# A two-layer transformer kernel: layer 1's cross attention and routing carried inside the full attention's steps

## The reference, cut to what matters

```python
h = _layernorm(x) * (1 + ca) + sa
x = x + ga * full_attention(h)            # 16 heads of 8, softmax over 1024 tokens
h = _layernorm(x) * (1 + cb) + sb
x = x + gb * ffn(h)

def ffn(hidden):                           # (S, B, H) = (4, 1024, 128)
    ln1 = layernorm(hidden) * w1 + b1
    q, k, v = split(ln1 @ qkv.T)           # 16 heads of 8 for q, 4 for k and v
    scores = einsum('sbhd,tbhd->bhst', q, k) / sqrt(8)      # over the leading axis, causal
    attn = einsum('bhst,tbhd->sbhd', softmax(scores), v)
    after = hidden + attn @ proj.T
    x = layernorm(after) * w2 + b2
    probs = softmax(x @ router.T)          # 8 experts, the best two taken
    ...                                    # gelu experts, weighted sum
    return after + moe_out
```

## Time and profile before

| What | Value |
|---|---|
| time, median of 3 runs | 2022.56 us (2022.13 to 2023.56) |
| the profiled execution | 2024.25 us, its span 2022.5 us |
| busy over the span | PE 1586.4, DVE 1386.9, ACT 1146.0, POOL 605.2 us |
| granted clock of PE, mean | 0.876 of full speed |
| full attention | 951.8 to 1632.7 us |
| double norm stage | 1633.9 to about 1694 us |
| cross and routing stage | 1696.5 to about 1871 us |
| experts and gather of layer 1 | 1871.4 to the end |

### The profile page before, as it was taken

One profiled execution on the slowest core, in us unless ns is written; L12 is line 12 of the kernel. 1 busy time (PEld: TensorE's weight loads), 2 busy tenths in 40 slices (PEclk: granted clock), 3 DMA queues, 4 the chain that ended last, 5 costly groups with the idle time before them and its releaser, 6 DMA issues. The chain is left out here.

```text
span 2022.5 us, 34560 instructions
## 1 busy us (share of the span) xinstructions
PE 1586.4 (78%) x11512; PEld 920.5 (46%) x11512; DVE 1386.9 (69%) x3531; ACT 1146.0 (57%) x2997; POOL 605.2 (30%) x670
## 2 busy tenths in 40 slices
PE   6799999999993399634999999999999953540780
PEld 3477877777772389622122222222222233440670
DVE  5655656656655164277999999999999656971653
ACT  3366666666662144343488888888888844210232
POOL 2133433633625377401001000100100011066574
PEclk8799999999996699866799999999999976555895
DMA  6144444411110467343000000000000000011664
GB/s 195 32 160 163 156 144 145 136 36 36 47 31 23 145 219 222 113 129 105 18 21 24 21 24 21 24 19 26 21 24 10 2 1 7 0 39 46 195 200 139
DMA packets 97805, 157.57 MB, mean 78 GB/s; under 512 B 18228, under 2 KB 64372, under 8 KB 97500
## 3 DMA queue, kind: packets, MB, share of 16 engines
q1 hardware_dynamic: 79900, 100.65, 17.1%
q0 software_dynamic: 17728, 54.71, 7.6%
HBM read 75.68 MB, written 63.49 MB: 69 GB/s over the span
## 5 line engine op out<-in xcount | busy, mean ns | idle before, releaser
L2106 DVE TENSOR_REDUCE q_max<-s_ps 128x1 f32<-128x1024 f32 x512 | 598.2, 1218 | 14.3 <-PE s_ps L1997 6.6
L2087 ACT ACTIVATE probs<-s_ps 128x512 f32<-128x512 f32 x1024 | 535.5, 603 | 124.9 <-PE s_ps L2018 124.7
L1997 PE MATMUL s_ps<-k_stack,q_stack 64*128 64x512 bf16 x1024 | 351.8, 397 | 17.5 <-PEq L99 9.1
L2018 PE MATMUL s_ps<-q_stack,k_stack 64*128 64x512 bf16 x1024 | 319.9, 385 | 20.1 <-ACT probs L2087 15.6
L2032 PE MATMUL o_ps<-probs,v_aug 128*32 128x512 f32 x2048 | 273.7, 607 | 0.7 <-ACT probs L2087 0.7
L2018 PEld LDWEIGHTS s_ps<-q_stack,k_stack 64*128 64x128 bf16 x1024 | 78.4, 94 | 334.4 <-ACT probs L2087 282.6
L1003 POOL TENSOR_TENSOR probs<-probs,p_rsum 128x512 f32<-128x512 f32 x128 | 132.9, 1039 | 311.5 <-DVE p_rsum L980 310.6
L883 ACT ACTIVATE probs<-s_biased,s_min 128x128 f32<-128x128 f32 (+1 forms) x512 | 197.7, 391 | 38.5 <-DVE s_min L974 37.1
L1638 POOL CAST neg_max_parts<-neg_max 16x128 bf16<-16x128 f32 x32 | 9.0, 281 | 475.0 <-DVE neg_max L2114 475.0
L748 PE MATMUL score_ps<-k_pad,q_bd 128*128 128x128 f32 x1024 | 146.0, 286 | 0.0
L974 DVE CUSTOM_DVE_ANT_0 s_biased<-score_ps,nbias 128x128 f32<-128x128 f32 (+1 forms) x512 | 115.7, 282 | 41.6 <-PE score_ps L748 40.4
(11 more groups left out here) (328 smaller groups left out, 2868.3 us busy)
## 6 DMA issues: line engine op xcount, KB each, us to landing
moe_rows<-zero_rows POOLq DMA_DIRECT2D x36, 975.0 KB, 5.9
moe0b_wblock<-in_L_ffn_blocks SPq DMA_DIRECT2D x39, 578.0 KB, 4.1
moe1b_wblock<-in_L_ffn_blocks SPq DMA_DIRECT2D x39, 256.0 KB
v_shift<-v_tiles SPq DMA_DIRECT2D x32, 256.0 KB, 3.4
v_shift<-v_tiles SPq DMA_DIRECT2D x32, 224.0 KB, 3.9
qk_parts_dram<-qk_parts SPq DMA_DIRECT2D x16, 384.0 KB, 2.6
q_stack<-qk_parts_dram SPq DMA_DIRECT2D x192, 32.0 KB
k_stack<-qk_parts_dram SPq DMA_DIRECT2D x192, 32.0 KB
```

The source lines that it names most:

```text
L1997: mm = nc.tensor.matmul(s1[u % 2][:, c * CH:(c + 1) * CH], qs[head_rows(m), quad % 4, j, qt * P:(qt + 1) * P], ks[head_rows(m), quad % 4, ...
L2018: nc.tensor.matmul(bank_of("exp", 4 * k + pos)[:], ks[head_rows(m), quad % 4, j, kt * P:(kt + 1) * P], qs[head_rows(m), quad % 4, j, half ...
L2087: nc.scalar.activation(pr[:, k % 2, HEADS[pos], :], bank_of("exp", n)[:], ACT.Exp).then_inc(sm["exp"], 1)
L2106: v.tensor_reduce(mx[:, h % 4, col:col + 1], s1[u % 2][:], AX.X, ALU.max).then_inc(sm["maxed"], 1)
```

## The change

`double_norm_stage` and `cross_route_stage` are removed. Their work becomes a class `BehindAttention`, made inside `full_attention_stage`, and every engine's loop over k gets a call `carried(k)`. For k in batch b (64 steps) it issues a part of the projection, the norms, the cross attention and the routing of batch b - 1, at fixed steps of the 64. Batch 3 follows behind the loop, in the same block. In detail:

- A `HalfNorm` replaces `Norm` and works on units of 4 tiles. In carried batches the odd tiles and the shift go to POOL.
- The cross attention of carried batches goes from DVE to POOL: the product (`score`), the sum over 8 as three halving additions, the totals and the weighted values. DVE keeps the maximum, the subtraction and the reciprocal. For batch 3 all of it is on DVE, in two halves of 4 tiles.
- Modulation of carried batches goes to POOL; for batch 3 it is on DVE.
- PE's turns, projections, logits and prefix counts use the ring of three `s2` banks: 18 further entries in `uses` a batch, 14 emptied by ACT and 4 by DVE.
- Logits and prefix counts are copied out of PSUM by ACT before DVE reads them.
- Scatters of a batch are spread over steps 61 to 70 after its batch's start of carrying (two a step, some in the next batch's steps); batch 3's 16 stand at the end.
- The weights are loaded by SP at the start of the attention stage (`C.load`). `q`, the scores and the products reuse spent buffers (`K.hT`, `K.mod_rows`).

More of the change, by code:

```diff
@@ L189, in affine @@
                                       ACT.Identity, bias=bias, scale=scale).then_inc(self.turn_read, 1)
[L192 to L281, removed]
@@ L1969, in split_max, with augment @@
                            nr[:])
-                wo.gate(pool)
-                for quad in range(NQ):
+                def augment(quad):
                     if quad >= 2:
@@ new lines, in total @@
+                def total(b):
+                    pool.wait_ge(C.exped, b + 1)
+                    if b == 0:
+                        g.tensor_copy(C.sm[:], C.sc[:, 0, :]).then_inc(C.totalled, 1)
+                    for t in range(1, b + 1):
+                        r = g.tensor_tensor(C.sm[:], C.sm[:] if t >= 2 else C.sc[:, 0, :], C.sc[:, t, :], ALU.add)
+                        if t < b:
+                            step(r)
+                        else:
+                            r.then_inc(C.totalled, 1)
@@ L1988, in _ @@
+                M1.wait_scattered(pool)
             @block.tensor
@@ L2225, in cross_route_stage @@
+class BehindAttention:
     QW, KW = H1 * HD1, KV2 * HD1
[L2226 to L2227 removed]
     R = H1 // KV2
[L2229 to L2501 removed]
@@ new lines, in attention_turned, with attention_product @@
+    def attention_turned(self, act, bank, u):
+        act.wait_ge(self.wo.turned, u + 1)
+        if u >= 2:
+            act.wait_ge(self.p_mm, u - 1)
+        self.nc.scalar.copy(self.aT[:, u % 2, :], bank[:]).then_inc(self.wo.t_out, 1)
+    def attention_product(self, pe, bank, u):
+        pe.wait_ge(self.wo.t_out, u + 1)
+        for i in range(CPT):
+            m = self.nc.tensor.matmul(bank[:, i * D:(i + 1) * D], self.aT[:, u % 2, i * P:(i + 1) * P],
+                                      self.wo.wg[:, u // 2, :], start=True, stop=True)
+        m.then_inc(self.wo.y_mm, 1)
@@ new lines, in project, with projected @@
+    def project(self, pe, bank, n):
+        pe.wait_ge(self.N2.turn_read, n // 2 + 1)
+        for i in range(2):
+            t = (2 * n + i) % TPB
+            m = self.nc.tensor.matmul(bank[:, i * QKV2:(i + 1) * QKV2], self.hT[:, t * P:(t + 1) * P], self.w[:],
+                                      start=True, stop=True)
+        m.then_inc(self.mm, 1)
+    def projected(self, act, bank, n):
+        act.wait_ge(self.mm, n + 1)
+        y = bank[:, 0:2 * QKV2].rearrange("p (t c) -> p t c", t=2)
+        if n % 4 == 0 and n >= 4:
+            act.wait_ge(self.below_max, n // 4)
+        self.nc.scalar.copy(self.q[:, 2 * n % TPB:2 * n % TPB + 2, :], y[:, :, 0:self.QW])
+        self.nc.scalar.copy(self.kv[:, :, 2 * n:2 * n + 2, :],
+                            y[:, :, self.QW:].rearrange("p t (a c) -> p a t c", a=2)).then_inc(self.qkv_out, 1)
@@ new lines, in exponentials, with out_turn, out_turned @@
+    def exponentials(self, act, b, ts, count):
+        act.wait_ge(self.below_max, count)
+        row = self.sc[:, 0:b + 1, self.columns(ts)]
+        self.nc.scalar.activation(row, row, ACT.Exp, scale=HD1 ** -0.5).then_inc(self.exped, 1)
+    def out_turn(self, pe, bank, u):
+        for i in range(CPT):
+            m = self.nc.tensor.transpose(bank[:, i * P:(i + 1) * P], self.at[:, u % 2 * CPT + i, :], self.K.ident[:])
+        m.then_inc(self.turned, 1)
+    def out_turned(self, act, bank, u):
+        act.wait_ge(self.turned, u + 1)
+        act.wait_ge(self.wo.y_mm, u + 1)
+        self.nc.scalar.copy(self.aT[:, u % 2, :], bank[:]).then_inc(self.t_out, 1)
@@ new lines, in out_product, with residual @@
+    def out_product(self, pe, bank, u):
+        pe.wait_ge(self.t_out, u + 1)
+        for i in range(CPT):
+            m = self.nc.tensor.matmul(bank[:, i * D:(i + 1) * D], self.aT[:, u % 2, i * P:(i + 1) * P], self.wp[:],
+                                      start=True, stop=True)
+        m.then_inc(self.p_mm, 1)
+    def residual(self, dve, bank, u):
+        dve.wait_ge(self.p_mm, u + 1)
+        h = self.K.nat[:, u * CPT:(u + 1) * CPT, :]
+        self.nc.vector.tensor_tensor(h, h, bank[:].rearrange("p (t d) -> p t d", d=D), ALU.add
+                                     ).then_inc(self.added, 1)
@@ new lines, in logits, with logits_out @@
+    def logits(self, pe, bank, b):
+        pe.wait_ge(self.N3.turn_read, 2 * (b + 1))
+        self.M.wait_router(pe)
+        for t in range(TPB):
+            m = self.nc.tensor.matmul(bank[:, t * E:(t + 1) * E], self.hT[:, t * P:(t + 1) * P], self.M.wg[:],
+                                      start=True, stop=True)
+        m.then_inc(self.M.logits_ready, 1)
+    def logits_out(self, act, bank, b):
+        M = self.M
+        act.wait_ge(M.logits_ready, b + 1)
+        if b >= 1:
+            act.wait_ge(M.placed, b)
+        self.nc.scalar.copy(M.raw[:], bank[:, 0:TPB * E].rearrange("p (t e) -> p t e", e=E)).then_inc(M.logit_mm, 1)
```

740 lines of the change are left out of this document (450 added, 290 removed).

## The result

The changed kernel takes 1968.8 us (median of 4 runs, 1966.8 to 1977.6), the kernel before 2023.1 on the same chip: ratio 0.974, 95% interval 0.971 to 0.977. Forecast were 1978 and a gain of 45; the gain is 54. The profiled execution's span went from 2022.5 to 1968.4.

The account below looks back on a forecast made before the run. Two full attention loops, DVE's reductions and PE with ACT, plus 238.7 us of waiting behind them, were taken as the bound. Tail -138.1 and attention +93.1 gave -45.0: 1978 us, own range 1960 to 1996, 8 in 10 1948 to 2006.

Parts of the forecast that it names:

- What goes: From the attention's last write to the expert stage's entry: all 238.7 us, for four batches, disappear.
- Behind the attention: After the attention only batch 3's projection, norms, cross attention, routing and scatters remain: 100.6 us to the experts' entry.
- Inside, per batch: Work carried in the next batch's 64 attention steps adds 33.6 us a batch, 93.1 in all after batch 2's router saving.
- DVE's four units: In carried attention steps, two projection and two output products emptied by DVE cost 1.25 us each, 5.0 a batch.
- projections: In carried attention steps, four projection units emptied by ACT lengthen the step by one copy, 0.58 us each.
- the give: Slack between the attention's DVE loop and PE/ACT loop, 0.4 us per alternation, taking 1.5 us off a batch.
- ACT's even tiles: In carried attention steps, six pairs of norm tiles on ACT at about 0.55 us each; with the exponentials 4.0 a batch.
- Batch 2's router in the last 12 steps: At the attention's end, batch 2's routing work of 7.7 us falls where DVE is free, so it costs nothing.
- Overlap: Rival in the attention: DVE's additions give PE and ACT time for theirs; +58 instead of +93, 1943 us; chance 0.15.
- Late POOL: Rival: POOL's elementwise work inside the attention runs late and others wait; 25 us more, 2003 us; chance 0.17.
- The starving ring: Rival: carried units on the three score banks break the run-ahead, each costing up to a step; 2043 us; chance 0.05.
- The port: Rival: DVE stands for POOL's reads in the attention, about 109 us over three batches; 2087 us; chance 0.01.

Follow-up runs that it names:

- experiment 1: Changed kernel plus DVE reductions and ACT copies that nobody needs and that take no score bank, in the attention's first batch; 1975.4 us.
- experiment 3: Changed kernel with the norms' even tiles of batches 0 to 2 made by POOL and not by ACT; 1976.7 us.
- experiment 5: Changed kernel with the four product units of batches 0 to 2 one step earlier, emptied by ACT and added by POOL; 1967.6 us, ratio 0.972.
- experiment 2: Changed kernel plus extra units on the score banks, emptied by ACT or DVE, and bank-free extra work, in the attention's first batch; 1977.4 us.
- experiment 4: Changed kernel with POOL making each product of queries and keys twice in batches 0 to 2; 1976.3 us.
- its second profile: The changed kernel itself, unchanged, run again on the same chip beside later edits; 1968.4 us, ratio 0.973.
- the version with the edits of 5 and 6: Changed kernel with ACT emptying product units and POOL adding, plus POOL taking last-batch score and value groups and spreading late scatters; 1966.4 us, 0.972.
- the three edits that moved real work: Changed kernel with ACT emptying product units, POOL helping DVE in the last batch, and DVE's carried work spread over more steps; 1965.2 us, 0.971.
- experiment 8: Version with all three work-moving edits plus unread score passes in the last 12 steps, 1962.1 us; with further filler passes behind the attention, 1960.6 us.

## Why the prediction was right, and by how much its steps were off

The mechanism was right: the time behind the attention goes for all but one batch, and inside it what is carried adds to a step, since both loops are full. The span shrank by 54.1 for 45.0. The difference is nearly all in one term, the attention: 82.3 for 93.1.

- *What goes*, 238.7: as read.
- *Behind the attention*, 100.6: 101.8. Norm 1's aggregates stood at 5.6 behind the last division (5.6 predicted), norm 2's at 13.2 (13.0), scores began at 19.5 (19.5) and ended at 33.3 (33.4), values ended at 46.9 (46.9), norm 3's statistics at 54.0 (52.8), slots at 70.2 (69.4); sixteen scatters 20.2 (20.2), entry 11.1 (11.0; the 2.2 in it for the semaphores stood on no row, only the sum of the two is measured). The one error is the output's turn, product and statistics: 7.1 for 5.9.
- *Inside, per batch*, 33.6, term by term against the steps of batch 1, whose sum is 29.1. It came as near as it did because errors of both signs met: statistics, even tiles and affine together 14.0, measured 9.6; softmax's maximum and reciprocal 1.85, measured 0.7 (0.8 and 1.3 in the later batches, with more rows); router and prefix 8.15, measured 7.1; DVE's four units 5.0, measured 4.9; turns 2.4, measured 2.15; projections 2.3, measured 3.2; logits 1.3, measured 1.56 (half of 3.58, from which the 1.3 was said to come, is 1.79); and the give, -1.5, which is inside the measured ones.
- The term that was mis-sized most is "ACT's even tiles: six pairs of 0.82 against the 0.33 that ACT idles per step, 0.55 each ... 4.0". Work of ACT that takes no bank does not queue on PE's loop: experiment 1 has 0.61 us of it for 0.08 and for nothing beside DVE's, experiment 3 the tiles of two norms for 0.4. For the third norm's tiles no run has the price.
- The second is how the give was counted: I took 0.4 off four times a batch. Experiment 1 has 0.35 to 0.4 off at every step with DVE work, and a batch has some fifteen such steps. What DVE did in one step beyond that adds in full: "DVE is full, so all of it counts" was right for large pieces and wrong for small ones.
- Undersized: the projections. Each has two copies on ACT and 192 columns a tile on PE, and costs 0.79; I had priced it as one copy. Experiment 5 has the same for products, 0.88 to 1.08 where a turn costs 0.58. So the price of a unit is not the copy alone; that what PE needs for it shows too fits both, and is not shown by a run of its own.
- Batch 2's router in the last 12 steps: 7.7 free predicted; the last batch's sum is 23.0 for 29.0, 6.6 less in the router and 0.6 more in the softmax.
- *Rivals.* Overlap: 1943 would have needed 35 less; experiments 1 and 2 exclude it. Late POOL: it had 0.4 us left in batch 2 (experiment 4); the power on four columns took 1.05 on average, not the 1646 ns of eight that the rival feared. The starving ring: 0.58 and 1.26 a unit, excluded. The port: DVE's reductions kept their length beside POOL's 22 busy us in 100:

```profile
L2246 DVE TENSOR_REDUCE q_max<-s_ps 128x1 f32<-128x1024 f32 x512 | 598.7, 1216 | 41.4 <-PE s_ps L2047 37.6
...
L2495 POOL TENSOR_TENSOR n1bb_rstd<-n1bb_ve,neghalf 128x4 f32<-128x4 f32 x8 | 8.4, 1056 | 12.1 <-DVE n1bb_ve L2490 12.1
```

- What I had said the profile would show, with what it shows: products 3.0 to 3.1 apart on average in batches 1 to 3 (2.98, 2.99 and 2.88, 2.95 on average; 2.53 in batch 0), so below what I said, and batch 3 is even under the 2.9 that was to be the sign of overlap; it is there because its router is nearly free, and experiments 1 and 2 answer the rival better than that average; the scatters' last issue some 90 behind the last division (89.8); DVE's waits for POOL under 1 us (0.64 behind the attention); the clock at half from the last division on (1.00 to 1720, then 0.50 to 0.73).

Not settled: why the clock fell in a router's steps in one execution and not in another of the same instructions. The changed kernel has it in batch 2, its second profile in batch 1 (0.6 us each), experiment 5 in both (about 2 us each), the version with the edits of 5 and 6 in batch 2 (0.6), and experiments 1 and 2 in neither. It is seen where PE had waited about 1.2 us for DVE, but such waits also pass without it. In the changed kernel's profile this score pass, at step 58 of batch 2, was followed by a product of 1.93 us; in its second profile the same one, behind a wait of 1.17, by a product of 1.06:

```profile
1510.13 0.39 PE L2047 MATMUL s_ps<-k_stack,q_stack 64*128 64x512 bf16 x1 [1.16 <-DVE q_max L2246]
```

## What to carry to other kernels

When two full loops share an in-order engine, price carried work by its engine and by what it takes: on the scarce ring its copy and PE's part of it, on the full engine its length less the give, off both nothing up to about half a microsecond a step; and lay it out in pieces no larger than the give, one a step, away from the step that already has a division. Read prices from a single step of a periodic stage, where two executions agree to 0.02 us, and not from the whole time. Where PE's work thins out at the end of a stage, compare the granted clock before anything else is tuned: passes that nobody reads brought 3.1 us there, and the three edits that moved real work 3.2 together.

## What the runs showed of the hardware

- **A wait of PE can cost twice.** After a wait of 1.30 us PE ran at 1.2 GHz for a little over 3 us inside a stage that otherwise holds 2.4 GHz (0.89 us), after the 4.6 us of experiment 4 for about as long (0.61 over 4 us). After waits of 1.17 it did so in some profiles and not in others; in the four with no wait above 0.73 in those steps it did not.
- **The clock can fall at small matmuls too.** The logits' sixteen passes of 8 columns in the last batch run where no score passes for maxima do. In six of the eleven profiles without the passes of experiment 8 the clock fell to 0.50, 1 to 3 us after the first of them: for 14 to 18 us in experiments 2, 3 and in all three edits together (4.6 to 6.0 us lost), for about 3.5 in 4, 5 and in 5 and 6 together (1.25 to 1.4 lost). In the other five, the changed kernel's two among them, it stayed at 1.00, and so it did in both versions with passes that nobody reads beside the scores. Why it falls in one execution and not in another is open. The logits themselves, first with all three edits, where the clock fell during them, then with the passes (timeline of PE):

```profile
1676.74 2.40 PE L2760 MATMUL s_ps<-moe_wg,hT 128*128 128x8 f32 x16
```

```profile
1678.24 1.95 PE L2762 MATMUL s_ps<-moe_wg,hT 128*128 128x8 f32 x16
```

- **Score passes of 64 rows beside others of 64 rows cost next to nothing**: the last 12 steps took 31.5 us with four more passes a step, 31.4 in the changed kernel.
- **DVE and POOL on two operands slow each other**: DVE's 128x512 product 0.69 alone, 0.94 and 1.08 beside POOL's; POOL's 1.79 beside DVE's, 1.28 while DVE waited; DVE's reduction 0.69 in both.
